# Attention scores of a two-map attention cut into four column tiles of TensorE, and the row maxima of both maps reduced in one instruction

## The reference, cut to what matters

```python
H, d = 16, 16;  scale = 1/sqrt(d)
q1, q2, k1, k2 = heads of x @ Wq1, x @ Wq2, x @ Wk1, x @ Wk2   # (B, H, S, d)
v = heads of x @ Wv                                             # (B, H, S, 2d)
a1 = softmax(where(causal, q1 @ k1.T * scale, -inf))
a2 = softmax(where(causal, q2 @ k2.T * scale, -inf))
out = (a1 - lam[h] * a2) @ v                                    # then a norm over 2d, and @ Wo
```

## Time and profile before

| | us |
|---|---|
| median of 3 runs | 3744.49 (3737.36 to 3744.53) |
| the profiled execution's own time | 3742.78 |
| its span | 3740.9 |
| PE busy | 3322.9 (89%) |
| DVE busy | 2753.5 (74%) |
| ACT busy | 2340.6 (63%) |
| POOL busy | 1691.1 (45%) |

### The profile page before, as it was taken

The page is one execution under the profiler, slowest core; times in us unless marked ns, Lnnn a source line. Parts: engine busy times, 40 slices in busy tenths (PEclk is TensorE's granted clock), DMA queues, the critical chain, the costliest instruction groups (busy, mean ns, idle before and its releaser), DMA issues. The chain is left out here.

```text
span 3740.9 us, 68222 instructions
## 1 busy us (share of the span) xinstructions
PE 3322.9 (89%) x22302; PEld 2021.6 (54%) x22302; DVE 2753.5 (74%) x6822; ACT 2340.6 (63%) x4989; POOL 1691.1 (45%) x2994
## 2 busy tenths in 40 slices
PE   6997999999999999999999968999699969969840
PEld 4774444444444444444444427888567746647740
DVE  6876999999999999999999934666545458733348
ACT  4663677777777777777777755776544445524432
POOL 2511366666666666666666660111000025546542
PEclk9998999999999999999999989999899979979975
DMA  6888434434443343334434303221242133244558
GB/s 210 256 257 206 76 74 77 81 71 74 80 77 72 75 79 75 73 77 78 73 73 79 61 15 107 85 85 63 65 127 65 46 111 104 96 144 152 151 183 253
DMA packets 380343, 393.47 MB, mean 105 GB/s; under 512 B 121368, under 2 KB 294424, under 8 KB 377816
## 3 DMA queue, kind: packets, MB, share of 16 engines
q1 hardware_dynamic: 365688, 350.56, 38.2%
q0 software_dynamic: 13728, 37.77, 2.7%
q10 hardware_dynamic: 576, 0.79, 0.1%
HBM read 230.21 MB, written 157.15 MB: 104 GB/s over the span
## 5 line engine op out<-in xcount | busy, mean ns | idle before, releaser
L732 ACT ACTIVATE att_p<-att_st 128x512 f32<-128x512 f32 (+3 forms) x3072 | 1325.4, 492 | 472.4 <-PE att_st L669 453.1
L799 DVE TENSOR_REDUCE att_mcol<-att_ring 128x1 f32<-128x512 f32 (+3 forms) x3072 | 1483.4, 547 | 137.4 <-PE att_ring L647 108.5
L669 PE MATMUL att_st<-att_ops 99*128 99x512 bf16 (+3 forms) x3072 | 913.6, 327 | 4.3 <-ACT att_p L732 3.5
L644 PE MATMUL att_ring<-att_ops 96*128 96x512 bf16 (+3 forms) x3072 | 877.3, 330 | 28.5 <-DMA att_va<-values 24.3
L681 PE MATMUL att_pv<-att_p,att_va 128*32 128x512 f32 (+3 forms) x6144 | 602.3, 494 | 2.2 <-POOL att_p L788 1.3
L788 POOL TENSOR_SCALAR_AFFINE_SELECT att_p<-att_p 128x512 f32<-128x512 f32 x512 | 321.7, 634 | 591.8 <-ACT att_p L732 587.0
L669 PEld LDWEIGHTS att_st<-att_ops 99*128 99x128 bf16 x3072 | 284.5, 98 | 445.4 <-ACT att_p L732 278.7
L647 PE MATMUL att_ring<-c_mask,c_identb 128*128 128x128 bf16 x2048 | 433.8, 221 | 0.0
L644 PEld LDWEIGHTS att_ring<-att_ops 96*128 96x128 bf16 x3072 | 296.3, 98 | 207.8 <-DVE att_mcol L799 81.0
L681 PEld LDWEIGHTS att_pv<-att_p,att_va 128*32 128x32 f32 x6144 | 144.1, 108 | 273.0 <-ACT att_p L732 140.4
L647 PEld LDWEIGHTS att_ring<-c_mask,c_identb 128*128 128x128 bf16 x2048 | 202.4, 99 | 106.2 <-issue 0.6
(11 more groups left out here) (285 smaller groups left out, 5973.6 us busy)
## 6 DMA issues: line engine op xcount, KB each, us to landing
att_ops<-parts SPq DMA_DIRECT2D x1524, 64.0 KB, 3.3
parts<-prj_pt SPq DMA_DIRECT2D x128, 384.0 KB, 4.1
moe_work<-moe_rows SPq DMA_DIRECT2D x79, 260.0 KB
values<-prj_vs SPq DMA_DIRECT2D x16, 1024.0 KB, 6.7
att_va<-values SPq DMA_DIRECT2D x64, 256.0 KB, 3.8
heads<-att_ofin SPq DMA_DIRECT2D x128, 128.0 KB, 2.4
ffn_os<-heads SPq DMA_DIRECT2D x16, 1024.0 KB, 4.8
moe_work<-x SPq DMA_DIRECT2D x32, 512.0 KB
```

Source lines behind the costliest of these rows:

```text
L644: ins = nc.tensor.matmul(ring[k % NB][:, 0:w], ops[0:KR, s, a, mp, i * P:(i + 1) * P], ops[0:KR, s, a, 2 + mp, c * GN:c * GN + w], start=T ...
L669: nc.tensor.matmul(stp[(t * NST + n) % NS][:, off:GN], ops[:, s, a, 2 + mp, j * P:(j + 1) * P], ops[:, s, a, mp, half * GN + off:(half + 1 ...
L732: act.activation(pr[:, g % R, b, off:GN], stp[(t * NST + n) % NS][:, off:GN], ACT.Exp, scale=SCALE).then_inc(exp_done, 1)
L799: v.tensor_reduce(mcol[:, t % 2, c, col:col + 1], ring[k % NB][:, 0:min(GN, (i + 1) * P - c * GN)], AX.X, ALU.max).then_inc(ring_read, 1)
```

## The change

It does four things. (1) `in_tiles` issues each matmul of `max_item` (the mask's too) and of `scores` as four, each with 32 of the 128 columns of weights, all moving columns, and a column tile of its own. (2) An item of the ring is now the same block of both maps of a head: 24 items in place of 48, each written to a buffer of two banks (NB = 2 buffers of (P, 2, 512)), and one reduction takes both maxima. (3) The transposes write the first bank of a buffer. (4) The tables of slots are others. The transposes stay as they were, in the whole array.

```diff
-    R, NB, NS = 6, 4, 3
+    R, NB, NS = 6, 2, 3
-    ITEMS = [(a, mp, i, c) for a in range(2) for mp in range(2) for k in range(HB)
-             for i, c in ((HB + k, 0), (k, 0), (HB + k, 1))]
+    ITEMS = [(a, i, c) for a in range(2) for k in range(HB) for i, c in ((HB + k, 0), (k, 0), (HB + k, 1))]
-    for before, step in ((35, ("turn", 0)), (6, ("rows", 0)), (4, ("turn", 1))):
+    for before, step in ((18, ("turn", 0)), (2, ("rows", 0)), (0, ("turn", 1))):
         RING.insert(before, step)
-    RING_AT = [20, 22, 22, 22, 24, 25, 25, 26, 28, 29, 30, 31, 33, 34, 34, 37, 37, 37, 39, 39, 40, 41, 42, 42, 46, 47,
-               47, 47, 48, 49, 49, 50, 51, 52, 53, 53, 54, 55, 55, 57, 59, 60, 60, 60, 61, 61, 64, 65, 65, 67, 67]
-    PV_AT = [10, 10, 15, 21, 27, 27, 35, 35, 38, 44, 48, 48]
-    COPY_AT = [35, 48]
+    RING_AT = [23, 24, 28, 29, 30, 30, 33, 35, 36, 37, 38, 40, 41, 44, 47, 49, 51, 52, 54, 56, 57, 58, 60, 62, 65, 65, 68]
+    PV_AT = [11, 15, 20, 24, 27, 30, 34, 36, 38, 45, 50, 53]
+    COPY_AT = [35, 56]
-        ring = [m.ps(f"ring{i}") for i in range(NB)]
+        ring = [m.ps(f"ring{i}", (P, 2, GN)) for i in range(NB)]
+            def in_tiles(out, stationary, moving, start=True, stop=True):
+                for row in range(0, P, VC):
+                    ins = nc.tensor.matmul(out[row:row + VC], stationary[:, row:row + VC], moving, start=start, stop=stop, tile_position=(0, row))
+                return ins
             def max_item(t, n):
-                a, mp, i, c = ITEMS[n]
+                a, i, c = ITEMS[n]
...
-                ins = nc.tensor.matmul(ring[k % NB][:, 0:w], ops[0:KR, s, a, mp, i * P:(i + 1) * P],
-                                       ops[0:KR, s, a, 2 + mp, c * GN:c * GN + w], start=True, stop=not diag)
-                if diag:
-                    ins = nc.tensor.matmul(ring[k % NB][:, w - P:w], C["identb"][:], C["mask"][:], start=False, stop=True)
+                for mp in range(2):
+                    ins = in_tiles(ring[k % NB][:, mp, 0:w], ops[0:KR, s, a, mp, i * P:(i + 1) * P], ops[0:KR, s, a, 2 + mp, c * GN:c * GN + w], stop=not diag)
+                    if diag:
+                        ins = in_tiles(ring[k % NB][:, mp, w - P:w], C["identb"][:], C["mask"][:], start=False)
                 ins.then_inc(ring_ready, 1)
             def scores(t, n):
...
-                nc.tensor.matmul(stp[(t * NST + n) % NS][:, off:GN], ops[:, s, a, 2 + mp, j * P:(j + 1) * P],
-                                 ops[:, s, a, mp, half * GN + off:(half + 1) * GN], start=True, stop=True).then_inc(st_ready, 1)
+                in_tiles(stp[(t * NST + n) % NS][:, off:GN], ops[:, s, a, 2 + mp, j * P:(j + 1) * P],
+                         ops[:, s, a, mp, half * GN + off:(half + 1) * GN]).then_inc(st_ready, 1)
             def reduce_item(t, n):
...
-                v.tensor_reduce(mcol[:, t % 2, c, col:col + 1], ring[k % NB][:, 0:min(GN, (i + 1) * P - c * GN)],
-                                AX.X, ALU.max).then_inc(ring_read, 1)
+                v.tensor_reduce(mcol[:, t % 2, c].rearrange("p (h i) -> p h i", i=SB)[:, 2 * a:2 * a + 2, i],
+                                ring[k % NB][:, :, 0:min(GN, (i + 1) * P - c * GN)], AX.X, ALU.max).then_inc(ring_read, 1)
```

More of the change, by code:

```diff
@@ L653, in max_rows @@
                 pe.wait_ge(ring_read, k - NB + 1)
-                nc.tensor.transpose(ring[k % NB][0:NM, 0:P], mcol[:, t % 2, 0], C["ident"][:]).then_inc(ring_ready, 1)
+                nc.tensor.transpose(ring[k % NB][0:NM, 0, 0:P], mcol[:, t % 2, 0], C["ident"][:]).then_inc(ring_ready, 1)
             def turn_sums(t, x):
@@ L661, in turn_sums @@
                 for b in range(HB):
-                    ins = nc.tensor.transpose(ring[k % NB][:, b * P:(b + 1) * P], ot[:, x, b * P:(b + 1) * P], C["ident"][:])
+                    ins = nc.tensor.transpose(ring[k % NB][:, 0, b * P:(b + 1) * P], ot[:, x, b * P:(b + 1) * P], C["ident"][:])
                 ins.then_inc(ring_ready, 1)
@@ L795, in reduce_item @@
             def reduce_item(t, n):
-                a, mp, i, c = ITEMS[n]
-                k, col = RING_NO["max", t, n], (2 * a + mp) * SB + i
+                a, i, c = ITEMS[n]
+                k = RING_NO["max", t, n]
                 v.wait_ge(ring_ready, k + 1)
-                v.tensor_reduce(mcol[:, t % 2, c, col:col + 1], ring[k % NB][:, 0:min(GN, (i + 1) * P - c * GN)],
-                                AX.X, ALU.max).then_inc(ring_read, 1)
+                v.tensor_reduce(mcol[:, t % 2, c].rearrange("p (h i) -> p h i", i=SB)[:, 2 * a:2 * a + 2, i],
+                                ring[k % NB][:, :, 0:min(GN, (i + 1) * P - c * GN)], AX.X, ALU.max).then_inc(ring_read, 1)
                 if n == NI - 1:
@@ L815, in max_parts @@
                     v.wait_ge(mp_ready, t)
-                v.tensor_scalar(mneg[:, 0], ring[k % NB][0:NM, 0:P], -1.0, None, ALU.mult).then_inc(ring_read, 1)
+                v.tensor_scalar(mneg[:, 0], ring[k % NB][0:NM, 0, 0:P], -1.0, None, ALU.mult).then_inc(ring_read, 1)
                 v.wait_ge(ring_read, k + 1)
@@ L832, in norm @@
                     v.wait_ge(ring_read, RING_NO["turn", t - 1 + x, 1 - x] + 1)
-                o = ring[no % NB][:].rearrange("p (b m w) -> p b m w", b=HB, m=4)
+                o = ring[no % NB][:, 0].rearrange("p (b m w) -> p b m w", b=HB, m=4)
                 nch.link(v.reciprocal(rl[:], o[:, :, :, VR]))
```

## The result

The changed kernel takes 3767.0 us (median of 4 runs), the kernel before beside it 3742.1: **ratio 1.0066, 95% interval 1.0047 to 1.0085**. It is slower by 25 us, where I forecast 75 us faster. The profiled execution has a span of 3768.7 us against 3740.9.

What follows compares the result with a forecast made beforehand. TensorE was taken as the bound in the attention loop, DVE 7% below. 62.06 pairs x 1.19 = 73.9 us, plus 1.6 before the loop, made 75 off: 3668 us, range 3645 to 3795, the forecast's own 3645 to 3700.

Steps and rivals of the forecast that it cites:

- Quads cost what their columns cost: Scores, maxima and masks on PE: four column tiles run beside each other, nothing extra; bounded above at 0.03 us each.
- short quads paced by issue: Rival, PE's 128-column quads: each needs 0.10 us, net +0.83 us per pair, 3792 us; chance 0.12.
- 0.06 us per matmul: Rival, PE's issue: 617 matmuls take 37.0 us per pair instead of 28.58, 4264 us; chance 0.02.
- 0.03 per quad: Rival, all 128 quads on PE: each pays a first pass's extra, +2.65 us per pair, 3906 us; chance 0.07.
- half speed: Rival, score and mask streams on PE: tiles don't keep bf16 speed, +16.6 us per pair, about 4770 us; chance 0.03.
- loads are hidden: Weight loads of quads on PE: hidden; the rival had each quad wait some 0.1 us, 4461 us, chance 0.02.
- Fewer shape changes: PE in the loop: full-array islands between column tiles fall from 8 to 3, saving 1.19 us per pair.
- Two double buffers for four single ones: PE's wait for DVE at the ring: taken as 0, bounded at nothing to 0.9 us per pair.
- the backlog sum: PE's and DVE's work added slot by slot over RING_AT: DVE's backlog stays under 0.85 us, less than one wide item.
- POOL's order is unchanged: POOL's queue, under moved steps and their queues: order stays, no DMA is added, no term in the sum.
- 1.6 us of gain: Before the loop, where the first pair's 48 reductions run alone: 24 double-width ones save 1.6 us.
- the coarser ring gives much of it back: Rival, PE waiting at the ring: 0.9 us of waits per pair leave 0.29 of gain, 3723 us; chance 0.10.

Runs made afterwards that it cites:

- e1: The kernel before with column tiles alone for scores, maxima and masks, old slots and single banks: 3687.5 us, ratio 0.9845.
- e3: The changed kernel with POOL's scaling of the first sums one diagonal group earlier (SCALE_AT 1 for 2): 3717.7 us, ratio 0.9933.
- e9: The changed kernel without POOL's power operation, so the norm's factor is missing from the result: 3649.9 us, ratio 0.9915.
- e5: The changed kernel's slots with single items on four single banks, and POOL's scaling one group earlier: 3654.0 us, ratio 0.9914.
- e2: The changed kernel's slots with each double item split in two single ones, four single banks, one reduction per map: 3747.5 us, ratio 1.0017.
- e8: The changed kernel with new tables of slots laid out from measured durations and POOL's scaling one group earlier: 3630.7 us, ratio 0.9858.
- e7: The kernel before with column tiles and single banks, and new tables of slots laid out from measured durations: 3576.7 us, ratio 0.9709.

## Why the prediction was wrong, by its own steps

**Right: the tiles.** Quads cost what their columns cost (0.22 and 0.06 us). All four rivals that made them dearer are out: short quads paced by issue, 0.06 us per matmul, 0.03 per quad, half speed; and loads are hidden. "Fewer shape changes", 1.19 us per pair, is borne out: e1's period is 0.93 us shorter. Its three islands cost 0.26, 0.29 and 0.21 instead of eight at 0.24, which is 1.14, and its ring waits grew from 0.27 to 0.45 us.

**Wrong: "Two double buffers for four single ones", taken at 0, bounded at 0.9 us per pair.** The four ring waits are 1.55. Put into the prediction's own sum they give the measured period: 28.58 - 1.19 + 1.55 = 28.94, and 28.96 was measured. The step that failed is the backlog sum, which said that DVE's backlog stays under 0.85 us and no item has to wait. It failed in two ways. DVE's split of maxima takes 1.33 us from its start to the next reduction in the trace of before (1008.08 to 1009.41) and 2.09 at its new place (1021.13 to 1023.22), and the wait behind it is 0.79 us. The sum had no such lengthening; durations of an operation were carried to a place where another engine does something else at the time. The other 0.76 us (0.39, 0.29 and 0.07) stay when nothing is held (e3, e9), and nearly as much stays with four single banks (0.31, 0.30 and 0.08 in e5). So they come from the new slots, and the sum overlooked them for a reason that no run here shows.

**Wrong by omission: "POOL's order is unchanged".** That is true and was not the question. The step asked in which queue each moved instruction stands, and not beside what it runs. The turn of maxima moved from slot 26 to 29 and POOL's scaling stayed in its order, and so they met. The kernel before had escaped it by 0.19 us.

**The sizes**, from the tiles alone (e1, loop 1767.0) to the changed kernel (1845.6), 79 us: 27 for slots, order of blocks and the earlier scaling (e5), 5.5 for the grain of the ring (e3), 46 for the meeting with POOL. Taken the other way round, through e2, the grain is 10.8 and the meeting 41. Before the loop the grain costs 6 to 7 us more (e3 and e5, the changed kernel and e2), where I had 1.6 us of gain. On the first 48 blocks PE's clock is low (0.50, and 0.61 in the kernel before) and PE needs twice as long per item (0.42 us for 512 columns, 375.16 to 375.58 in the kernel before). DVE is busy 28.4 us of 36 in place of 34.5, which I read as the engines taking turns with two buffers. The clock also stays at 0.50 until 399 us, where in the kernel before it is 1.00 from 389 on. How much each of the two costs isn't shown.

**The rival nearest to it**, "the coarser ring gives much of it back", had the place (PE idle released by DVE at the ring above 0.5 us per pair) and too low a price, and it named the wrong reason: single banks at the same slots wait nearly as long (e2). None of my rivals had a change of DVE's durations. On DVE's side the saving was real, 0.06 us for each pair of blocks (two wide reductions of the changed kernel start 1.14 us apart, 1014.14 and 1015.28, and two single ones take 1.20), and in the loop it bought nothing, as the prediction said.

**A misreading without effect.** The prediction pairs the second copy (slot 0 to 8) with "its turn (7 to 9)". By the tables that is the turn of the first sums; the second sums are turned in slot 23 of the next pair, before in 24. No wait of the runs hangs on it.

Left open are how the 27 us of slots divide, and why PE waits at the wide items of slots 41 and 44.

## What to carry to other kernels

When a step moves in a schedule written by hand, list what the other engines do in the same microsecond, not only what stands in its own queue: DVE's small steps took two to four times as long beside POOL here. Look also for meetings that the kernel before only just escapes. Where a change brings several things, try the one on the bounding engine alone first: the tiles with the old tables kept 59 us of the 74 that I had summed for the loop, and the new tables lost them. The changed kernel with one number changed went from 0.7% slower to 0.7% faster, with new tables to 1.4% faster (e8), and single banks with new tables to 2.9% (e7).

## What the runs showed of the hardware

DVE's small steps with SBUF on both sides are held by POOL's long operations on SBUF until these end: a cast of 0.21 us took 0.52, a subtraction of 0.28 took 0.73, each ending some 0.1 us after POOL's. In the changed kernel a subtraction was held when POOL's scaling started 0.03 to 0.09 us ahead of it (0.66 to 0.73 us), and not when it started 0.09 us later (0.28). Reductions that read PSUM ran on unheld beside the same POOL operations (512 columns in e1: 0.68 us beside the scaling, beside the mask and beside neither, the medians). The Trainium skill has this (SBUF — State Buffer, "Who interferes with whom"): DVE and GpSimd share a pair of ports under an exclusive lock, taken by casts in some modes and by operations with two SBUF inputs. The traces agree for the scaling and the mask. They don't for POOL's power operation (8 columns, 1.67 us by the profile, whose spans of POOL are rough): in the kernel before both casts and both subtractions ran beside it (1008.39 to 1009.48, the power operation from 1007.92 to 1009.59) in their usual 0.21 and 0.28 us, and in the changed kernel the first cast did.

Four bf16 column tiles run beside each other at the rate of one whole-array matmul, their weight loads hidden, also at 128 columns: 0.06 us for four, and 617 matmuls in a period of 26.95 us with PE full (e7).

Going from column tiles to whole-array matmuls and back cost 0.21 to 0.29 us (e1).
